# Layer one's turns without a hardware loop, a join shared by ScalarE and VectorE, and layer two's weights composed earlier

## The chip, the cores and the metric

The kernel runs on one core of one Trainium2 chip, as one program with five instruction streams: TensorE (PE; its weight loads are shown apart as PEld), VectorE (DVE), ScalarE (ACT), GpSimd (POOL) and SyncE (SP). Each engine runs its stream in order, and they meet at semaphores. The metric is the device time of one execution in microseconds (us).

## What is computed

Two message-passing layers on a graph of 3125 nodes (160 features: 64 scalars, 32 vectors of 3) and 103125 edges, sorted by target node. All is float32. Layer one, with its constants left out:

```python
h = relu(layernorm(x))
h_s, h_v = s @ lin1_ws * a, einsum(v, lin1_wv) * a       # s, v: the parts of h
w = silu(edge_scalars @ fc_w1) @ fc_w2                    # 224 weights for each edge
es, ev = h_s[edge_src], h_v[edge_src]                     # a gather for each edge
mid = [w1*es*e0, w4*(ev.e1)], [w2*es*e1, w3*ev*e0, w5*cross(ev, e1)]
agg = segment_sum(mid, edge_dst)
pre = sc(h) + agg @ lin2
x = x + [silu(pre[:, :64]), sigmoid(pre[:, 64:96]) * pre_v]
```

Layer two does without edge weights: it gathers `h = relu(layernorm(x))` by edge, multiplies with the edge's four attributes and with W1 to W5, sums by target node, applies Ws and Wv, and returns `x + (x' + relu(...))`. Since all is linear between the gather and the last relu, W1 to W5 and Ws, Wv are composed on the chip into one block of weights.

## The kernel before

**Edges.** 128 edges are a tile, 7 tiles a group, 4 groups (`UNROLL`) a turn. There are 116 groups, so 29 turns (`ITERS`), and the last group holds one tile. A stage `o` of a turn works on the turn's group `o`; some work of a stage is for the group before or after it. `stages` (line 731) sets the order for PE, ACT and DVE: two turns written out (`LEAD`), a hardware loop `Fori` over 8 rounds of three turns (`PERIOD`, the turn's place in it is the phase `p`), and three turns written out. Within the loop the number of the turn is in a register, and so are the addresses in `rel` and `sh`. POOL's stream has all turns written out already.

**Gathers.** The source rows of a tile come to `g` in one of four ways. POOL's indirect DMA (line 894) fetches most tiles, 128 rows each; it may start on a group when the products of the group four before it are done (`prod_done`). In phases 0 and 1 the last tile of group 3 is fetched row by row, by SP in one and by ACT in the other (`fetch_rows`, line 779): ACT issues `SHARES` rows behind each stage, 12 in each, but 12, 12, 8 and none in phase 1. And in layer one the last tile of groups 0 and 2 (`PICKED0`) is *found*: DVE compares the edges' source numbers with all node numbers (`match_rows`, line 1016, 128x3200), PE multiplies the match with the whole table, held as an upper and a lower half (`find0`, line 1287, 25 matmuls, to `found_at` in `sums`), and DVE adds the two halves (`join0`, line 1035, a reduction) into `g`. This happens in stages 1 and 3 of a turn (`FIND0`), 54 times in all. PE waits for the join (`found_copied`) before it aggregates into the same bank.

**A stage of layer one.** On DVE: `select` (lines 996 and 1000: the one-hot of the target within a window of 32 nodes, times the four attributes), `join0`, the products with the edge weights (lines 1087 to 1101), `name_rows` and `match_rows`, `turn` (a transpose, line 1112) and `add` (line 1133: into the accumulator `acc0`, at an address loaded from `place_i`). On PE: find, edge weights (line 1230), hidden layer (line 1216), aggregation (line 1266, 56 matmuls) and once a turn `lin2` (line 1304). On ACT: the Silu of the hidden layer (line 920), once a turn a copy of lin2's result (line 928), and then the rows of `row_part`.

**Between the layers** (`tensor_mid`, `scalar_mid`, `vector_mid`, lines 1350 to 1453), 25 tiles of nodes go through transposes (PE, line 1356, four banks), a sigmoid (ACT, line 1375), two products (DVE, lines 1405 and 1408), an addition to `X` (POOL) and statistics (DVE). Then come the normalisation, the table of layer two to DRAM, its two halves (line 1443) and `windows`. At the end DVE multiplies `pair` and `wout` with their constants (lines 1448, 1449), PE composes five planes of weights (line 1365, into the four banks) and ACT copies them to `big1_sb` (line 1394). Layer two begins on ACT with a conversion of the names (line 935), for which DVE's first matching (line 1051) waits.

**The head** loads, in SP's order, the features, later `first_rows` (which waits for 7 gathered tiles), then `pair`, `pair_k`, `wout`, `wout_k` (lines 382 to 386). On DVE `vector_self` multiplies `big0_sb` (line 552), copies from `sums` (line 555) and makes the lower half of the table (line 558, 128x4000, both operands in SBUF).

## Time and profile before

| | |
|---|---|
| median of 3 runs | 1861.78 us (1860.4 to 1862.68) |
| profiled execution | 1865.19 us, its span 1863.4 us |
| busy: PE, DVE, POOL, ACT | 1714.3, 1685.2, 1339.0, 171.4 us |
| layer one, first to last operation of DVE | 53.5 to 976.0 us |
| between the layers | to 1028.0 us |
| layer two and the output | to the end |

Times are microseconds from the span's start. A row of a timeline is: start, duration, engine, line, operation, output <- inputs, shape, count, and in brackets the idle time before it with what ended it. An engine whose row shows no idle time in brackets was busy up to it, or idle by less than 0.15 us. The "granted clock" is TensorE's. Busy time leaves out what an engine's sequencer does alone: register operations, branches, waits, issues of DMAs.

### The profile page before, as it was taken

How to read it: one execution, taken by the hardware profiler on the slowest of the kernel's cores; microseconds unless marked ns; L12 is line 12 of the kernel's file. 1: busy time of each engine (PE TensorE's matmuls, PEld its weight loads, DVE VectorE, ACT ScalarE, POOL GpSimd, SP SyncE). 2: the span in 40 equal slices, each digit the busy share in tenths (PEclk: the TensorE clock that was granted, in tenths of full speed). 3: DMA queues.
4: the chain of work that ended last, by engine and by line, in shares of the span. 5: the costliest groups of instructions: out<-in, count | busy, mean ns of one | idle time of the engine just before them, and what ended most of it. 6: DMA issues, size and time to landing. Idle time of an engine off the chain costs nothing.

```text
span 1863.4 us, 57341 instructions
## 1 busy us (share of the span) xinstructions
PE 1714.3 (92%) x15973; PEld 1488.8 (80%) x15973; DVE 1685.2 (90%) x3031; ACT 171.4 (9%) x359; POOL 1339.0 (72%) x1424
## 2 busy tenths in 40 slices
PE   8999899989898989999983899999999999999997
PEld 6677676777676767777752899999999999999997
DVE  7999899989999999999988988989898989889896
ACT  6100000000000000000005000000000000000000
POOL 4777777777777777777755777777777777777774
PEclk9899999999999999999995999999999999999999
DMA  8344443443434343434422333333333333333333
GB/s 278 105 106 108 108 110 96 107 106 98 118 91 110 102 109 103 108 91 116 112 75 86 78 84 76 83 75 84 82 76 80 83 75 82 75 81 83 74 84 90
DMA packets 109737, 181.03 MB, mean 97 GB/s; under 512 B 30072, under 2 KB 74480, under 8 KB 109248
## 3 DMA queue, kind: packets, MB, share of 16 engines
q0 software_dynamic: 66672, 113.88, 25.6%
q1 hardware_dynamic: 35592, 60.39, 10.4%
q10 hardware_dynamic: 7112, 2.94, 0.7%
q8 instruction: 106, 1.74, 0.4%
q14 instruction: 255, 2.09, 0.4%
HBM read 170.37 MB, written 6.72 MB: 95 GB/s over the span
## 4 chain that ended last, share of the span: by engine, by line
DVE 36%; PE 28%; issue 23%; ACTq 6%; DVEq 6%; DMA 1%; ACT 0%; POOL 0%; POOLq 0%
PE w_ps L1294 10%; DVE arena L1093 10%; DVE arena L1087 6%; DVE match L1051 5%; ACTq L779 5%; PE sums L1266 3%; PE sums L1270 3%; DVEq L1118 3%; PE sums L1304 3%; DVE mixed L996 3%; PE w_ps L1230 3%; DVE turned L1112 2%; PE hid_ps L1216 2%; DVE arena L1101 2%; DVE sel L1000 1%
## 5 line engine op out<-in xcount | busy, mean ns | idle before, releaser
L894 POOL DMA_INDIRECT g<-node_table,src x1382 | 1314.3, 951 | 462.1 <-issue 405.9
L1294 PE MATMUL w_ps<-split,match 128*128 128x320 f32 x3325 | 531.4, 318 | 7.9 <-DVE match L1051 7.4
L1294 PEld LDWEIGHTS w_ps<-split,match 128*128 128x128 f32 x3325 | 504.0, 193 | 12.0 <-DVE match L1051 12.0
L1051 DVE TENSOR_TENSOR match<-hid_ps,node_id_sb 128x3200 fp32r<-128x3200 f32 x105 | 361.4, 3456 | 6.9 <-ACT hid_ps L935 6.9
L1093 DVE TENSOR_TENSOR arena<-w_ps,g 128x384 f32<-128x384 f32 (+3 forms) x693 | 296.7, 455 | 2.0 <-DMA g<-node_table 1.3
L1266 PEld LDWEIGHTS sums<-arena,sel 128*32 128x32 f32 x6448 | 203.8, 111 | 116.5 <-DVE sel L1000 57.9
L1230 PE MATMUL w_ps<-fc_sb,arena 64*128 64x224 f32 x1612 | 226.9, 382 | 56.2 <-DVE arena L1087 29.5
L1000 DVE TENSOR_TENSOR sel<-mixed,sh 128x896 f32<-128x896 f32 x232 | 251.5, 1084 | 27.2
L1270 PE MATMUL sums<-g,sel 128*128 128x160 f32 x1612 | 241.5, 300 | 24.0 <-DMA g<-node_table 21.9
L1266 PE MATMUL sums<-arena,sel 128*32 128x160 f32 x6448 | 245.8, 303 | 18.0 <-DVE g L1035 17.9
L1270 PEld LDWEIGHTS sums<-g,sel 128*128 128x128 f32 x1612 | 227.2, 190 | 26.6 <-DMA g<-node_table 24.1
L1230 PEld LDWEIGHTS w_ps<-fc_sb,arena 64*128 64x128 f32 x1612 | 167.4, 193 | 100.2 <-DVE arena L1087 56.0
L1287 PE MATMUL sums<-split,match 128*128 128x320 f32 x1350 | 212.6, 313 | 0.0
L1287 PEld LDWEIGHTS sums<-split,match 128*128 128x128 f32 x1350 | 198.4, 188 | 13.6 <-issue 13.6
L1016 DVE TENSOR_TENSOR match<-mixed,node_id_sb 128x3200 fp32r<-128x3200 f32 x54 | 188.1, 3484 | 0.9
L1087 DVE TENSOR_TENSOR arena<-w_ps,g 128x256 f32<-128x256 f32 x462 | 155.6, 376 | 0.0
L1216 PE MATMUL hid_ps<-arena,fc_sb 128*128 128x512 f32 x232 | 136.2, 670 | 1.8 <-issue 1.8
L920 ACT ACTIVATE arena<-hid_ps 128x512 f32<-128x512 f32 x116 | 69.4, 598 | 740.7 <-PE hid_ps L1216 553.2
L996 DVE TENSOR_TENSOR mixed<-mixed,rel 128x224 f32<-128x224 f32 x232 | 89.4, 386 | 37.3 <-issue 30.2
L1112 DVE STREAM_TRANSPOSE turned<-sums 128x160 f32<-128x160 f32 x232 | 78.3, 338 | 26.0 <-PE sums L1304 23.1
L1051 DVE TENSOR_TENSOR match<-mixed,node_id_sb 128x3200 fp32r<-128x3200 f32 x28 | 97.8, 3492 | 1.0
L1060 DVE TENSOR_REDUCE g<-w_ps 128x160 f32<-128x320 f32 x133 | 62.5, 476 | 17.6 <-PE w_ps L1294 17.6
(113 smaller groups left out, 793.0 us busy)
## 6 DMA issues: line engine op xcount, KB each, us to landing
g<-node_table SPq DMA_DIRECT2D x2304, 0.6 KB
g<-node_table ACTq DMA_DIRECT2D x2304, 0.6 KB
arena<-edge_feat_dram SPq DMA_DIRECT2D x60, 512.0 KB
g<-node_table,src POOLq DMA_INDIRECT x1382
named<-src_rows_dram SPq DMA_DIRECT2D x30, 320.0 KB
named<-src_rows_dram SPq DMA_DIRECT2D x30, 128.0 KB
X<-x_dram SPq DMA_DIRECT2D x5, 400.0 KB, 6.5
sh<-edge_sh_dram SPq DMA_DIRECT2D x1, 1624.0 KB, 9.2
```

The lines of the kernel that those rows point to most:

```text
L894: nc.gpsimd.indirect_dma_start(out=g[:, slot(p, u, j), :], out_offset=None, in_=table[layer], in_offset=bass.IndirectOffsetOnAxis(ap=src[: ...
L1000: nc.vector.tensor_tensor(sel[:, o % 2, 0:n, :].rearrange("p t (k n) -> p t k n", k=4), hot[:, 0:n, :].unsqueeze(2).to_broadcast([P, n, 4, ...
L1016: nc.vector.tensor_tensor(match0[:], wanted0[:, i, :].unsqueeze(1).to_broadcast(wide), node_id_sb[:].unsqueeze(2).to_broadcast(wide), ALU. ...
L1051: nc.vector.tensor_tensor(match[MATCH_OF[i]][:], wanted_of[i].unsqueeze(1).to_broadcast(wide), node_id_sb[:].unsqueeze(2).to_broadcast(wid ...
L1087: return nc.vector.tensor_tensor(blocks(at), w[:, :, h * S_CH:(h + 1) * S_CH].rearrange("p t (m c) -> p t m c", m=2), rows[:, :, 0:S_CH].r ...
L1093: nc.vector.tensor_tensor(blocks(at), w[:, :, 2 * S_CH + j * V_CH:2 * S_CH + (j + 1) * V_CH].unsqueeze(2).to_broadcast([P, n, m, V_CH]), r ...
L1216: nc.tensor.matmul(hid_ps[:], fc1_sb[:], feat[:, half, within * HID:(within + 1) * HID], start=True, stop=True).then_inc(hid_done, 1)
L1230: last = nc.tensor.matmul(w_ps[:, h, part[2 * h + j] - a, 0:W_N], hid[at, o % 2, (2 * h + j) * P:(2 * h + j + 1) * P], fc2_sb[at, :], tile ...
L1266: last = nc.tensor.matmul(sums[at, o % 2, 0:width].rearrange("p (m n) -> p m n", n=WIN), sel[:, o % 2, j, at], row, tile_position=(0, k * ...
L1270: last = nc.tensor.matmul(sums[:, o % 2, 0:D], sel[:, o % 2, j, :], g[:, slot(p, o % UNROLL, j), :], **first_last)
L1287: last = nc.tensor.matmul(found_at, match0[:, t, :], split0[:, :, t, :], start=(t == 0), stop=(t == NT - 1))
L1294: last = nc.tensor.matmul(banks[:, BANK_OF[i], 0:2 * D], match[MATCH_OF[i]][:, t, :], split[:, t, :], start=(t == 0), stop=(t == NT - 1))
```

## The change

1. `WRITTEN_OUT` names layer one: `stages` writes out its 29 turns in Python for PE, ACT and DVE, with no loop inside a pass. The number of the turn and the addresses that hang on it are constants. Layer two keeps its loop. The streams grow: DVE's from 1501 to 3701 rows of the listing.
2. The join is in two parts. ACT's new `put` runs first in each stage of layer one: it waits for `found` and for the products that last read the tile's place, and copies the upper half from PSUM to `g`. DVE's `join0` waits for ACT's `upper_copied` and adds the lower half.
3. The four loads of layer two's weights are issued before `first_rows`, and DVE multiplies them in `vector_self`. PE composes one plane behind the transposes of tiles 4, 8, 12, 16 and 20 into the banks of `sums`; ACT copies each two gates later.

```diff
@@ -63,6 +63,8 @@
 PIECES = ((0, 2), (BY_ACT, 15), (2, 5), (15, 18), (5, 8), (18, 22), (8, BY_ACT), (22, NT))
 THIRD = 3
 
+COMPOSED_AT = (4, 8, 12, 16, 20)
+
@@ -88,6 +90,8 @@
 PERIODS = ITERS // PERIOD
 assert LEAD == PERIOD - 1
 ROW_TILES = (2, 2)
+
+WRITTEN_OUT = (0,)
 PARTS = (48, 48, 32)
 SHARES = ((12,) * 8 + (12, 12, 8, 0),) * 2
 AT_ONCE = 12
@@ -378,12 +382,12 @@
                 sp.wait_ge(rows_ready, b)
                 sp.dma_start(table_v[0][:, a:b, :], H[:, a:b, :]).then_inc(rows_out, 16)
             load_feat(sp, 1, 1)
-            sp.wait_ge(first_ready, RAW)
-            sp.dma_start(first_rows, g[:, 0:RAW, :].rearrange("p t c -> p (t c)")).then_inc(first_out, 16)
             sp.dma_start(pair[:], l1_pair).then_inc(pair_in, 16)
             sp.dma_start(pair_k[:], l1_pair_scale).then_inc(pair_in, 16)
             sp.dma_start(wout[:], l1_out).then_inc(pair_in, 16)
             sp.dma_start(wout_k[:], l1_out_scale).then_inc(pair_in, 16)
+            sp.wait_ge(first_ready, RAW)
+            sp.dma_start(first_rows, g[:, 0:RAW, :].rearrange("p t c -> p (t c)")).then_inc(first_out, 16)
             sp.sem_inc(first_back, 1)
             sp.wait_ge(turns_set, 1)
 
@@ -550,6 +554,9 @@
         def vector_self(dve):
             dve.wait_ge(big0_in, 32)
             nc.vector.tensor_tensor(big0_sb[:], big0_sb[:], big0_k, ALU.mult).then_inc(big0_ready, 1)
+            dve.wait_ge(pair_in, 64)
+            nc.vector.tensor_tensor(pair[:], pair[:], pair_k[:], ALU.mult)
+            nc.vector.tensor_tensor(wout[:], wout[:], wout_k[:], ALU.mult).then_inc(weights_ready, 1)
             for j, at in enumerate(CHUNK_N):
                 dve.wait_ge(sc_done[1], j + 1)
                 nc.vector.tensor_copy(acc0[:, 1, at], sums[0:S_OUT, SC_BANK[1][j], 0:at.stop - at.start]).then_inc(sc_ready[1], 1)
@@ -676,6 +683,7 @@
             late_copied = sem(L + "late_copied")
             match_done = sem(L + "match_done")
             found = sem(L + "found")
+            upper_copied = sem(L + "upper_copied")
             found_copied = sem(L + "found_copied")
             pass_of = {}
 
@@ -735,6 +743,14 @@
 
                 pass_of[eng] = r
                 q = eng.snap(ITERS * r)
+                if layer in WRITTEN_OUT:
+                    for it in range(ITERS):
+                        f = eng.snap(q + it)
+                        k, p = divmod(it - LEAD, PERIOD) if it >= LEAD else (-1, it - LEAD)
+                        e = eng.snap(PERIODS * r + max(k, 0)) - (it < LEAD)
+                        for s in range(UNROLL * it, UNROLL * (it + 1) if it < ITERS - 1 else last):
+                            stage(f, it, s - UNROLL * it, s, p, e, k)
+                    return
                 e = eng.snap(PERIODS * r + 0) - 1
                 for it in range(LEAD):
                     f = eng.snap(q + it)
@@ -927,6 +943,22 @@
                         act.wait_ge(acc_done, UNROLL * f)
                     nc.scalar.activation(lin_out, lin_ps, ACT.Copy).then_inc(lin2_copied, 1)
 
+                def put(f, o, s):
+
+                    if s == 0:
+                        act.sem_inc(upper_copied, 1)
+                    if not found0_at(o, s):
+                        return
+                    i, nxt, made = found0_at(o, s)
+                    n = NP0 * nxt + i
+                    if made:
+                        act.wait_ge(found, NP0 * f + (n + 1))
+                        act.wait_ge(prod_done, 2 * UNROLL * f + 2 * (UNROLL * nxt + PICKED0[i] + 1 - UNROLL))
+                        nc.scalar.activation(g[:, slot(-1, PICKED0[i], TILES - 1), :], found_at[:, 0, :], ACT.Copy).then_inc(upper_copied, 1)
+                    else:
+                        act.wait_ge(upper_copied, NP0 * f + n)
+                        act.sem_inc(upper_copied, 1)
+
                 def cast_early(f, nxt):
 
                     act.wait_ge(named_in[layer], 16 * f + (16 * nxt + 16))
@@ -945,7 +977,7 @@
 
                 def row_part(f, it, o, s, p, e, k):
 
-                    if ROW_TILES[layer] < 2 or o >= UNROLL or p < -1 or (p == PERIOD - 1 and s is not None):
+                    if ROW_TILES[layer] < 2 or o >= UNROLL or p < -1 or isinstance(it, int) and it == ITERS - 1:
                         return
                     part = (p + 1) % PERIOD
                     tile = e if part else e + 1
@@ -959,7 +991,9 @@
                         load_by_row(act, 1, k + 1)
 
                 def stage(f, it, o, s, p, e, k):
-                    if not own_weights:
+                    if own_weights:
+                        put(f, o, s)
+                    else:
                         if s == 0:
                             cast_early(f, 0)
                             cast_late(f, 0)
@@ -1031,9 +1065,9 @@
                     i, nxt, made = found0_at(o, s)
                     n = NP0 * nxt + i
                     if made:
-                        dve.wait_ge(found, NP0 * f + (n + 1))
-                        nc.vector.tensor_reduce(g[:, slot(-1, PICKED0[i], TILES - 1), :], found_at.rearrange("p h c -> p c h"),
-                                                AXX, ALU.add).then_inc(found_copied, 1)
+                        dve.wait_ge(upper_copied, NP0 * f + (n + 1))
+                        to = g[:, slot(-1, PICKED0[i], TILES - 1), :]
+                        nc.vector.tensor_tensor(to, to, found_at[:, 1, :], ALU.add).then_inc(found_copied, 1)
                     else:
                         dve.wait_ge(found_copied, NP0 * f + n)
                         dve.sem_inc(found_copied, 1)
@@ -1348,6 +1382,20 @@
             return e
 
 
+        def compose(pe, m):
+
+            if m == 0:
+                pe.wait_ge(weights_ready, 1)
+            if m >= 2:
+                pe.wait_ge(comp_copied, m - 1)
+            for c in range(2):
+                last = nc.tensor.matmul(sums[:, m % 2, 0:D], pair[:, 2 * m + c, :], wout[:, c, :], start=(c == 0), stop=(c == 1))
+            last.then_inc(comp_done, 1)
+
+        def composed(act, m):
+            act.wait_ge(comp_done, m + 1)
+            nc.scalar.activation(big1_sb[:, m, :], sums[:, m % 2, 0:D], ACT.Copy).then_inc(comp_copied, 1)
+
         def tensor_mid(pe):
             for t in range(NT):
                 if t >= BANKS:
@@ -1356,15 +1404,9 @@
                     last = nc.tensor.transpose(banks[:, t % BANKS, r * S_OUT:(r + 1) * S_OUT], acc0[:, r, t * P:(t + 1) * P],
                                                ident_sb[0:S_OUT, 0:S_OUT])
                 last.then_inc(node0_done, 1)
+                if t in COMPOSED_AT:
+                    compose(pe, COMPOSED_AT.index(t))
             pe.wait_ge(val_ready, NT)
-            pe.wait_ge(weights_ready, 1)
-            for m in range(PLANES[1]):
-                if m >= BANKS:
-                    pe.wait_ge(comp_copied, m - BANKS + 1)
-                for c in range(2):
-                    last = nc.tensor.matmul(banks[:, m % BANKS, 0:D], pair[:, 2 * m + c, :], wout[:, c, :],
-                                            start=(c == 0), stop=(c == 1))
-                last.then_inc(comp_done, 1)
             pe.wait_ge(comp_copied, PLANES[1])
 
         def scalar_mid(act):
@@ -1378,6 +1420,8 @@
             nc.scalar.activation(warm[:], zero[:], ACT.Sigmoid)
             for t in range(NT):
                 gate(t)
+                if t - 2 in COMPOSED_AT:
+                    composed(act, COMPOSED_AT.index(t - 2))
             root(act, parts[0], 0, var1_step, root1_done)
             act.wait_ge(norm1_ready, 1)
             root(act, parts[1], 1, var1_step, root1_done)
@@ -1389,9 +1433,6 @@
             act.wait_ge(h1_by_dve, len(by_dve))
             nc.scalar.activation(split[:, BY_ACT:, 0:D], H[:, BY_ACT:, :], ACT.Copy).then_inc(upper_ready, 1)
             nc.scalar.activation(acc[1][:, 0, :], zero[0:ROWS[1], :].to_broadcast([ROWS[1], ACC_W]), ACT.Copy).then_inc(acc1_clear, 1)
-            for m in range(PLANES[1]):
-                act.wait_ge(comp_done, m + 1)
-                nc.scalar.activation(big1_sb[:, m, :], banks[:, m % BANKS, 0:D], ACT.Copy).then_inc(comp_copied, 1)
 
         def vector_mid(dve):
             n = 0
@@ -1444,9 +1485,6 @@
             last.then_inc(split_ready, 1)
             then = Steps(dve, edge_set)
             windows(then)
-            dve.wait_ge(pair_in, 64)
-            nc.vector.tensor_tensor(pair[:], pair[:], pair_k[:], ALU.mult)
-            nc.vector.tensor_tensor(wout[:], wout[:], wout_k[:], ALU.mult).then_inc(weights_ready, 1)
             dve.wait_ge(acc1_clear, 2)
             dve.wait_ge(split_ready, 1)
             dve.wait_ge(rows1_out, 16 * len(pieces))
```

DVE in stage 1 of a turn of layer one. Before, within the loop (line 996 is the one-hot, 1035 the join, 1093 the first product):

```order
L1112 STREAM_TRANSPOSE turned<-sums 128x160 [waits l0_agg_done]
L996 ISA [waits l0_sel_done,l0_agg_done]
L996 TENSOR_TENSOR mixed<-mixed,rel 128x224
L999 REGISTER_ALU
L1000 ISA [waits l0_hot_done]
L1000 TENSOR_TENSOR sel<-mixed,sh 128x896
L1034 REGISTER_ALU
L1035 TENSOR_REDUCE g<-sums 128x160 [waits l0_found]
L1066 REGISTER_ALU
L868 ISA [waits l0_w_done]
L1093 TENSOR_TENSOR arena<-w_ps,g 128x4x96 [waits l0_gathered10]
```

After:

```order
L1146 STREAM_TRANSPOSE turned<-sums 128x160 [waits l0_agg_done]
L1030 TENSOR_TENSOR mixed<-mixed,rel 128x224 [waits l0_sel_done,l0_agg_done]
L1033 REGISTER_ALU
L1034 TENSOR_TENSOR sel<-mixed,sh 128x896 [waits l0_hot_done]
L1068 REGISTER_ALU
L1070 TENSOR_TENSOR g<-g,sums 128x160 [waits l0_upper_copied]
L1100 REGISTER_ALU
L884 ISA [waits l0_w_done]
L1127 TENSOR_TENSOR arena<-w_ps,g 128x4x96 [waits l0_gathered10]
```

The separate `ISA` ahead of the one-hot and of line 1000 are gone, and the reduction that waited for `found` is an addition that waits for `upper_copied`.

ACT at the end of stage 2's rows and the start of stage 3, before (line 779 issues a row, 920 is the Silu):

```order
L779 ISA
L779 DMA g<-node_table 1x160
L917 REGISTER_ALU
L919 REGISTER_ALU [waits l0_hid_done]
L920 ACTIVATE arena<-hid_ps 128x512 [waits l0_w_done]
L776 TENSOR_LOAD by_row
```

After (line 795 issues a row, 936 is the Silu):

```order
L795 ISA
L795 DMA g<-node_table 1x160
L955 REGISTER_ALU
L957 ACTIVATE g<-sums 128x160 [waits l0_prod_done,l0_found]
L933 REGISTER_ALU
L935 REGISTER_ALU [waits l0_hid_done]
L936 ACTIVATE arena<-hid_ps 128x512 [waits l0_w_done]
L792 TENSOR_LOAD by_row
```

The copy of the upper half (line 957) stands between the last row of the stage before and the Silu.

PE behind the last transposes between the layers, before, up to the entry of layer two:

```order
L1356 MATMUL w_ps<-ident_sb,arena 128x96 [waits val_ready]
L1356 MATMUL w_ps<-ident_sb,arena 128x96
L1365 MATMUL w_ps<-wout,pair 128x160 [waits weights_ready,val_ready]
L1365 MATMUL w_ps<-wout,pair 128x160 x7
L1365 MATMUL w_ps<-wout,pair 128x160 [waits comp_copied]
L1365 MATMUL w_ps<-wout,pair 128x160
L723 TENSOR_LOAD turns_i [waits comp_copied]
```

And after, at the first of the five compositions (line 1404 is the transpose, 1392 the composition):

```order
L1404 MATMUL w_ps<-ident_sb,arena 128x96 [waits val_ready]
L1404 MATMUL w_ps<-ident_sb,arena 128x96
L1392 MATMUL sums<-wout,pair 128x160 [waits weights_ready]
L1392 MATMUL sums<-wout,pair 128x160
L1404 MATMUL w_ps<-ident_sb,arena 128x96 [waits val_ready]
```

The ten matmuls stood together behind all transposes; now two of them stand behind the transposes of every fourth tile.

DVE in the head, after:

```order
L552 COPY mixed<-iota_sb 128x32 [waits iota_in,place_step]
L556 TENSOR_TENSOR big_sb<-big_sb,arena 128x960 [waits big0_in,place_step]
L558 TENSOR_TENSOR pair<-pair,pair_k 128x1280 [waits pair_in]
L559 TENSOR_TENSOR wout<-wout,wout_k 128x320
L562 COPY arena<-sums 96x512 [waits sc_done1] x6
L562 COPY arena<-sums 96x128 [waits sc_done1]
L565 TENSOR_TENSOR split_49<-nodes,split_49 128x4000 [waits upper0_ready,rows_out]
```

The two multiplications (lines 558 and 559) are new at this place; before, line 552's product of `big_sb` was followed at once by the copies from `sums`.

## Rows read from the trace of the kernel before

**Rows 1.** Page, busy time: us, share of the span, instructions of each engine.

```profile
PE 1714.3 (92%) x15973; PEld 1488.8 (80%) x15973; DVE 1685.2 (90%) x3031; ACT 171.4 (9%) x359; POOL 1339.0 (72%) x1424
```

**Rows 2.** Waits, DVE, 60 to 980 us: us in total, times, longest us.

```profile
DVE mixed L996 <- issue: 19.9, 6, 3.6
DVE mixed L996 <- PE sums L1266: 6.2, 18, 3.1
```

**Rows 3.** Timeline, POOL's gathers, then DVE's last full group of layer one.

```profile
33.50 0.94 POOL L894 DMA_INDIRECT g<-node_table,src  x1 [8.70 <-DMA node_table<-nodes]
...
50.10 4.27 POOL L894 DMA_INDIRECT g<-node_table,src  x1 [0.30 <-issue]
...
199.88 0.95 POOL L894 DMA_INDIRECT g<-node_table,src  x1 [0.31 <-issue]
...
333.76 0.94 POOL L894 DMA_INDIRECT g<-node_table,src  x1 [0.30 <-issue]
...
961.53 0.95 POOL L894 DMA_INDIRECT g<-node_table,src  x1 [0.30 <-issue]
...
1841.17 0.95 POOL L894 DMA_INDIRECT g<-node_table,src  x1 [0.30 <-issue]
...
972.77 0.71 DVE L1093 TENSOR_TENSOR arena<-w_ps,g 128x288 f32<-128x288 f32 x2
```

**Rows 4.** Timeline, DVE's matchings in the loop's last turn and behind it.

```profile
861.13 3.48 DVE L1016 TENSOR_TENSOR match<-mixed,node_id_sb 128x3200 fp32r<-128x3200 f32 x1
...
877.30 3.49 DVE L1016 TENSOR_TENSOR match<-mixed,node_id_sb 128x3200 fp32r<-128x3200 f32 x1
...
892.83 3.48 DVE L1016 TENSOR_TENSOR match<-mixed,node_id_sb 128x3200 fp32r<-128x3200 f32 x1
...
908.75 3.49 DVE L1016 TENSOR_TENSOR match<-mixed,node_id_sb 128x3200 fp32r<-128x3200 f32 x1
...
924.01 3.48 DVE L1016 TENSOR_TENSOR match<-mixed,node_id_sb 128x3200 fp32r<-128x3200 f32 x1
```

**Rows 5.** Groups by line and form: busy us, mean ns of one, idle before.

```profile
L1087 DVE TENSOR_TENSOR arena<-w_ps,g 128x192 f32<-128x192 f32 x230 | 70.0, 344 | 0.0
...
L1035 DVE TENSOR_REDUCE g<-sums 128x160 f32<-128x320 f32 x54 | 25.8, 479 | 0.0
...
L1394 ACT ACTIVATE nodes<-w_ps 128x160 f32<-128x160 f32 x5 | 1.5, 304 | 11.0 <-PE w_ps L1365 11.0
```

**Rows 6.** Timeline, stage 3: DVE's join and ACT's next operation, two turns.

```profile
888.63 0.48 DVE L1035 TENSOR_REDUCE g<-sums 128x160 f32<-128x320 f32 x1
...
889.28 0.60 ACT L920 ACTIVATE arena<-hid_ps 128x512 f32<-128x512 f32 x1 [5.33 <-PE hid_ps L1216]
...
919.81 0.48 DVE L1035 TENSOR_REDUCE g<-sums 128x160 f32<-128x320 f32 x1
...
921.03 0.60 ACT L920 ACTIVATE arena<-hid_ps 128x512 f32<-128x512 f32 x1 [5.63 <-PE hid_ps L1216]
```

**Rows 7.** Waits, POOL, 60 to 960 us, then 1030 us to the end.

```profile
POOL g L894 <- DVE arena L1087: 21.8, 28, 3.2
...
POOL g L894 <- PE sums L1270: 16.2, 35, 3.1
```

**Rows 8.** DMA issues: KB each, median us from issue to landing.

```profile
wout_k<-l_out_scale_dram SPq DMA_DIRECT2D x1, 160.0 KB, 8.5
...
arena<-x_node_dram,src POOLq DMA_INDIRECT x7, 3.7
```

**Rows 9.** Timeline, the head's copies, and the end of the stretch between the layers.

```profile
43.82 0.69 DVE L555 COPY arena<-sums 96x512 f32<-96x512 f32 x1 [3.61 <-PE sums L613]
...
1019.18 1.49 DVE L1448 TENSOR_TENSOR pair<-pair,pair_k 128x1280 f32<-128x1280 f32 x1
...
1021.22 4.75 PE L1365 MATMUL w_ps<-wout,pair 128*128 128x160 f32 x20 [23.12 <-DVE wout L1449]
...
1027.97 10.29 DVE L1051 TENSOR_TENSOR match<-hid_ps,node_id_sb 128x3200 fp32r<-128x3200 f32 x3 [6.89 <-ACT hid_ps L935]
```

## The prediction

> **What bounds the kernel now.** I read first the busy times of the engines: TensorE (PE) 92%, VectorE (DVE) 90%, GpSimd (POOL) 72% of the span [rows 1]. None is idle enough to be ignored, so I read who waits for whom in layer one (60 to 980 us). There DVE waits almost only for its own instruction stream: 19.9 us in 6 waits ahead of the first operation of a group (line 996), the longest 3.6 us, and one more of 3.1 us that the view books under PE [rows 2]. Those seven are the seven returns of the hardware loop. So DVE paces layer one. PE does not: nearly all of its waits there are for DVE. But POOL is nearly as close as DVE. It issues gathers back to back: from 199.88 to 333.76 us there are 107 intervals, 1.251 us each, with no gap [rows 3]. Busy 72% hides that, since the 0.30 us between two gathers are not counted. In layer two PE paces, with POOL again close behind.
>
> **Returns of the loop.** The change writes out all 29 turns, so the seven returns go: 19.9 + 3.1 = 23.0 us of idle time, less what the same operation waits anyway (the 17 other waits of the second row make 3.1 us, 0.18 each, so 1.3): **-21.7 us** on DVE. PE's and ACT's own returns lie beside DVE's.
>
> **Registers.** In the loop, the addresses of `rel` and `sh` come from a register, and an extra instruction stands ahead of lines 996 and 1000. The trace has one ordinary turn written out already, the first of the three that stand behind the loop. From matching to matching (line 1016) the loop takes 16.17 + 15.53 = 31.70 us a turn, and the written-out turn 15.92 + 15.26 = 31.18 us [rows 4]. 24 turns leave the loop: 24 x 0.52 = **-12.5 us** on DVE.
>
> **The join.** DVE's reduction of 128x320 takes 479 ns. It becomes an addition of 128x160. A product of 192 columns takes 344 ns [rows 5], so I take 0.31 us at 160 columns: 0.17 us less, 54 times, **-9.2 us** on DVE.
>
> **The wait that comes with the join.** DVE no longer waits for PE's `found`, which is 2.5 us old by then, but for ACT's copy. ACT works in order, and its copy stands behind the twelve row loads of the stage before. In stage 3 these end late: the next operation of ACT starts at 889.28 in a loop turn where DVE's join starts at 888.63; in the written-out turn it is 921.03 against 919.81 [rows 6]. The new copy takes the place of that operation. A copy of 128x160 out of PSUM takes 0.30 us [rows 5]. So the join would come 889.28 + 0.30 - 888.63 = 0.95 us late at the loop's pace, 1.2 us once DVE is 0.27 us faster between its two joins, and 921.03 + 0.30 - 919.81 = 1.5 us by the written-out turn. I take 1.4. It happens where stage 2 has twelve rows: in turns 1 to 26, except the nine of phase 1, which have eight rows there, so 18 times: **+25 us** (22 to 27). Stage 1's join has over 2 us to spare, since find ends well before it and the rows end at about the same time as find. Queued behind DVE's wait are the products of that group; PE waits for them. That makes the join's move a loss by itself, since 25 is more than 9.2.
>
> **DVE's path through layer one:** -21.7 - 12.5 - 9.2 + 25.2 = -18.2 us.
>
> **POOL's path.** The layer has 727 gathers, the first at 33.50, the last at 961.53 [rows 3]. 726 x 1.2512 = 908.4 us, so 19.6 of the 928.0 us are lost: 3.3 in the gather of 4.27 us at 50.10, 0.3 in one before it, and 16 in waits for buffers that DVE frees late (28 of them are booked under DVE, the longest 3.2 us [rows 7]). A faster DVE gives back these 16 us at most. The last full group's last gather then starts at about 945, and lands 3.7 us later by the first gathers of the program [rows 8], at 949. DVE's products of it start at 972.77 now [rows 3]. So POOL allows -23.8 us and no more: of the 43.4 us that DVE alone would save, 20 are not to be had whatever ACT does. DVE's -18.2 ends later, so it counts.
>
> **The head.** DVE now multiplies `pair` and `wout` (1.49 and 0.48 us, as the same operations take at 1019 us [rows 9]) ahead of the copies that start at 43.82 [rows 9]. The last of the four loads lands 8.5 us after its issue [rows 8]; issued behind the feature load, from 31.6 on, it lands at some 42.3, so DVE is free at 44.3: **+0.5 us** (0 to 3). The other effect is on POOL: the gather at 50.10 took 4.27 us instead of 0.95, while DVE ran one addition of 128x4000 with both operands in SBUF. The two multiplications are of that kind, so I count 1.0 us (0.3 to 1.7) for POOL, which is already in the 945 above. The Trainium skill ("SBUF — State Buffer", section "Who interferes with whom") says that a tensor_tensor with both inputs in SBUF contends only with GpSimd's reads and was not seen to stall descriptor generation; by that the 1.0 us would be nothing. The row at 50.10 speaks against it, and it would not change the path that ends last.
>
> **Between the layers.** Now DVE multiplies at 1019.18, PE composes, ACT copies, and only then does ACT convert the names for which DVE's first matching waits: it starts at 1027.97 [rows 9]. After the change ACT is free before DVE is, and DVE is free after its windows at 1019.2, so the first matching starts at about 1019.5: -8.5 us. The five compositions lie among 25 gates, where DVE paces and PE waits for DVE in every tile; each puts 4.75 / 5 = 0.95 us on PE [rows 9], which has a lead of three tiles: +0.3 us (0 to 1.5). Layer two, however, has the same floor: POOL starts as before, waits for PE 16.2 us in 35 waits [rows 7], of which 0.30 each is its ordinary gap, so 5.7 us can be given back, and 0.4 for the multiplication that slowed a gather at 1020. Its last gather starts at 1841.17 [rows 3], just ahead of the last full aggregation. So between 6.1 and 8.5: I take **-7.3 us**.
>
> **Sum:** -18.2 + 0.5 + 0.3 - 7.3 = -24.7 us. The profiled execution took 1865.19 us (span 1863.4), the median of the runs is 1861.78. The sum is made on the profile and taken from the median: **1837 us**.
>
> **Rivals.**
> *A, POOL paces.* ACT's copy isn't late, or only so little that DVE's path falls under POOL's. For it: at the loop's pace the lateness is 0.95 us, and below 1.1 us POOL's floor decides. Against it: the written-out turn shows more. Time: 1861.8 - 23.8 + 0.3 - 7.3 = 1831; with all of the 8.5 us, 1830.
> *B, ACT is later than I read.* When DVE waits for ACT and ACT's rows wait for PE, a delay can be handed round. With 2.2 us for each of 18 joins, layer one gives -43.4 + 40 = -3.8, and the whole -10: 1851.
> *C, slower.* The copy queues not only behind the rows but, in stage 1 too, behind the Silu that waits for PE. The point is 18 x w = 43.4 + 6.5 + 3.7, w = 3.0 us; at 3.3 us the time is 1861.8 - 43.4 + 59.4 - 6.5 = 1871. Against it: ACT's rows never end more than 1.3 us after the join in these rows.
> *D, the long code isn't free.* Streaming four times as many instructions stalls the engines and gives back the returns: around 1858, no difference that can be told. Against it: the tail's turn and POOL, whose code is written out already and whose interval never varies.
>
> **How the numbers follow.** My forecast (1832 to 1845) has 0.50, A with less than 1832 0.25, B 0.15, D 0.04, C 0.04, and 0.02 for a gain below both floors. 1828 to 1849 takes in the first two, the bounds of the unknown costs (ACT 22 to 27, between the layers 6.1 to 8.5, the head 0 to 3) and half of B. A measurement of this kernel tells 0.2% (3.7 us) from no change: faster 0.91, same 0.04, slower 0.05.
>
> **What would show it.** Idle time of 3 us ahead of DVE's first operation of a group is gone; a turn takes about 32.2 us where twelve rows precede and 30.8 elsewhere; DVE's addition waits for ACT some 18 times for 1.2 to 1.6 us; POOL waits for DVE next to nothing and its last gather of layer one starts at 946 to 950. If DVE instead waits for gathers in most turns, A holds. DVE's first matching of layer two follows its windows within 1 us, and the compositions are nowhere waited for. The forecast is wrong if a stall stands in the middle of written-out code, or if stage 1's addition waits too.

## Result and the profile after

The changed kernel takes 1837.83 us (median of 4 runs, 1834.34 to 1844.54), the kernel before 1861.68 us (4 runs, 1860.4 to 1862.68): a ratio of 0.9877, 95% interval 0.9848 to 0.9905. Run again beside other kernels it took 1838.46 us (below). 1837 was forecast.

The profiled execution of after took 1834.34 us, its span is 1832.4, so it is 31.0 us shorter than the profiled one of before, while the medians differ by 23.9. After's is the fastest of its runs, before's is slower than its other ones. The stages have to be compared with that in mind, and further down it matters.

The page of after, busy times, which answer to [rows 1]:

```profile
PE 1693.8 (92%) x15973; PEld 1477.0 (81%) x15973; DVE 1674.9 (91%) x3031; ACT 184.4 (10%) x413; POOL 1339.8 (73%) x1424
```

The shares say next to nothing: DVE is 91% busy instead of 90%. The waits say it. DVE from 60 to 960 us (us in total, times, longest), to be set against [rows 2]:

```profile
DVE g L1070 <- ACT g L957: 25.2, 18, 1.7
DVE arena L1167 <- DVE arena L1167: 4.6, 27, 0.5
DVE arena L1167 <- issue: 2.0, 3, 1.5
...
DVE arena L1127 <- DMA g<-node_table: 1.1, 1, 1.1
...
DVE mixed L1030 <- PE sums L1300: 0.3, 1, 0.3
```

The seven waits of 3 us ahead of the first operation of a group are gone. In their place stands the addition (line 1070), which waits 18 times for ScalarE's copy (line 957), 25.2 us in all. The costs of the join itself, by line and form (busy us, mean ns of one, idle before):

```profile
L1070 DVE TENSOR_TENSOR g<-g,sums 128x160 f32<-128x160 f32 x54 | 17.0, 315 | 25.5 <-ACT g L957 25.2
L957 ACT ACTIVATE g<-sums 128x160 f32<-128x160 f32 x54 | 16.4, 304 | 284.6 <-issue 129.9 <-PE sums L1321 127.4 <-DVE arena L1121 27.4
```

The turn, read from DVE's matchings in the timeline (start, duration), to be set against [rows 4]:

```profile
396.75 3.48 DVE L1050 TENSOR_TENSOR match<-mixed,node_id_sb 128x3200 fp32r<-128x3200 f32 x1
412.34 3.49 DVE L1050 TENSOR_TENSOR match<-mixed,node_id_sb 128x3200 fp32r<-128x3200 f32 x1
429.13 3.48 DVE L1050 TENSOR_TENSOR match<-mixed,node_id_sb 128x3200 fp32r<-128x3200 f32 x1
444.72 3.49 DVE L1050 TENSOR_TENSOR match<-mixed,node_id_sb 128x3200 fp32r<-128x3200 f32 x1
459.82 3.48 DVE L1050 TENSOR_TENSOR match<-mixed,node_id_sb 128x3200 fp32r<-128x3200 f32 x1
475.41 3.49 DVE L1050 TENSOR_TENSOR match<-mixed,node_id_sb 128x3200 fp32r<-128x3200 f32 x1
```

396.75 to 429.13 is a turn with twelve row loads ahead of the late copy, 32.4 us (32.2 forecast); 444.72 to 475.41 is one with eight, 30.7 us (30.8 forecast).

GpSimd no longer waits in layer one. All 26 entries below are its ordinary gap of 0.3 us, where [rows 7] had waits of up to 3.2:

```profile
POOL g L910 <- DVE arena L1121: 7.9, 26, 0.3
```

Timeline of after: GpSimd's gather beside DVE's long addition in the head, its last of layer one, its first and last of layer two; DVE's last full group of layer one, the first product of the gates, and the first matching of layer two. They answer to [rows 3] and [rows 9]:

```profile
48.80 5.40 POOL L910 DMA_INDIRECT g<-node_table,src  x1 [0.31 <-issue]
...
946.60 0.95 POOL L910 DMA_INDIRECT g<-node_table,src  x1 [0.30 <-issue]
992.61 1.68 POOL L910 DMA_INDIRECT g<-node_table,src  x1 [9.48 <-DMA node_table<-nodes]
...
1813.20 0.95 POOL L910 DMA_INDIRECT g<-node_table,src  x1 [0.30 <-issue]
...
952.70 0.71 DVE L1127 TENSOR_TENSOR arena<-w_ps,g 128x288 f32<-128x288 f32 x2
...
962.85 0.28 DVE L1446 SCALAR_TENSOR_TENSOR val<-w_ps,a_col,sig 128x64 f32<-128x64 f32 x1 [0.90 <-PE w_ps L1404]
...
999.86 10.29 DVE L1085 TENSOR_TENSOR match<-hid_ps,node_id_sb 128x3200 fp32r<-128x3200 f32 x3 [0.93 <-DVE place_i L539]
```

**Where the 31.0 us of the two profiled executions went.** The first product of the gates starts at 983.24 before and 962.85 after: layer one gave 20.4. From there the first matching of layer two follows after 44.73 us before and 37.01 after: the early composition gave 7.7. From that matching to the last gather both need 813 us (1027.97 to 1841.17, 999.86 to 1813.20). The last 3.0 us lie behind the last gather, and all of them ahead of the transposes of the output (before, then after; TensorE's rows from the last gather on):

```profile
1841.85 2.14 PE L1270 MATMUL sums<-g,sel 128*128 128x160 f32 x14 [0.67 <-DVE turned L1112]
1845.44 2.44 PE L1270 MATMUL sums<-g,sel 128*128 128x160 f32 x16 [1.45 <-DVE sel L1000]
...
1853.61 6.30 PE L1477 MATMUL w_ps<-ident_sb,nodes 80*128 80x80 f32 x50 [2.88 <-DVE nodes L1133]
```

```profile
1814.54 2.42 PE L1304 MATMUL sums<-g,sel 128*128 128x160 f32 x8 [2.22 <-DMA g<-node_table,src]
...
1822.69 4.92 PE L1515 MATMUL w_ps<-ident_sb,nodes 80*128 80x80 f32 x50 [2.57 <-DVE nodes L1167]
```

When the last gather starts, TensorE has 30 matmuls of aggregation left before and 8 after, so the transposes start 12.4 us behind it before and 9.5 after. They took 6.30 and 4.92 us, at a mean granted clock of 0.57 and 0.64 of full speed in ten microseconds, but that doesn't set the end: from their start to the end of the span it is 9.8 and 9.7 us, and in dve_join (below), where they took 6.29 us, 9.7 as well. In the two other kernels with the late composition they also start over 12 us behind the last gather (12.3 and 12.4), in those with the early one 9.1 to 11.2. So these 3 us belong to layer two's part of the change, which gave 10.6 in all between these two executions.

### The profile page after: what moved, and what is told of

It is laid out like the page before. It is cut to its first block, busy times and chain, and to the rows that moved or that the text cites. A ratio compares the mean times of both kernels' runs of the same rounds, so it can differ in the third digit from the quotient of the medians.

```text
span 1832.4 us, 57154 instructions
## 1 busy us (share of the span) xinstructions
PE 1693.8 (92%) x15973; PEld 1477.0 (81%) x15973; DVE 1674.9 (91%) x3031; ACT 184.4 (10%) x413; POOL 1339.8 (73%) x1424
## 4 chain that ended last, share of the span: by engine, by line
PE 29%; DVE 25%; issue 21%; ACTq 16%; DVEq 4%; ACT 2%; DMA 2%; POOL 1%; POOLq 0%
ACTq L795 13%; PE w_ps L1328 11%; DVE arena L1127 6%; DVE match L1085 5%; PE sums L1338 5%; PE sums L1300 4%; PE sums L1304 4%; DVE arena L1121 3%; ACTq L792 2%; DVEq L1152 2%; PE w_ps L1264 2%; DVE mixed L1030 2%; PE hid_ps L1250 2%; DVE turned L1146 2%; DVE arena L1135 1%
## 5 line engine op out<-in xcount | busy, mean ns | idle before, releaser
L1264 PE MATMUL w_ps<-fc_sb,arena 64*128 64x224 f32 x1612 | 221.0, 373 | 34.6 <-DVE arena L1121 31.1
L1304 PEld LDWEIGHTS sums<-g,sel 128*128 128x128 f32 x1612 | 227.9, 191 | 27.3 <-DMA g<-node_table 22.1
L1264 PEld LDWEIGHTS w_ps<-fc_sb,arena 64*128 64x128 f32 x1612 | 161.3, 187 | 78.3 <-DVE arena L1121 59.7
L1250 PE MATMUL hid_ps<-arena,fc_sb 128*128 128x512 f32 x232 | 131.5, 649 | 1.8 <-issue 1.8
L944 ACT ACTIVATE lin_sb<-sums 96x256 f32<-96x256 f32 (+1 forms) x58 | 22.1, 381 | 561.7 <-PE sums L1338 455.8
```

The lines of the kernel that those rows point to most:

```text
L1264: last = nc.tensor.matmul(w_ps[:, h, part[2 * h + j] - a, 0:W_N], hid[at, o % 2, (2 * h + j) * P:(2 * h + j + 1) * P], fc2_sb[at, :], tile ...
L1304: last = nc.tensor.matmul(sums[:, o % 2, 0:D], sel[:, o % 2, j, :], g[:, slot(p, o % UNROLL, j), :], **first_last)
```

## Experiments

Each is the changed kernel with one edit, or two. Times are medians; ratios are to the kernel before, run on the same chip beside it. "The copy waits" are the waits of DVE's line for ScalarE's copy in layer one.

| kernel | us | ratio (95%) | copy waits | first gate product | from there to the end |
|---|---|---|---|---|---|
| before | 1861.68 | 1 | none | 983.24 | 880.2 |
| after | 1837.83 | 0.9877 (0.9848 to 0.9905) | 25.2, 18 times | 962.85 | 869.6 |
| after_again | 1838.46 | 0.9875 (0.9852 to 0.9897) | 25.4, 18 | 963.39 | 870.8 |
| dve_join | 1833.66 | 0.9847 (0.9828 to 0.9866) | none | 959.55 | 869.4 |
| copy_between | 1830.41 | 0.9829 (0.9807 to 0.9851) | none | 957.63 | 870.8 |
| compose_late | 1840.12 | 0.9878 (0.9859 to 0.9897) | 25.6, 18 | 968.25 | 876.4 |
| dve_join_compose_late | 1834.43 | 0.9847 (0.9820 to 0.9873) | none | 957.06 | 874.9 |
| loop_kept | 1869.68 | 1.0044 (1.0027 to 1.0062) | 21.2, 18 | 999.39 | 870.5 |
| compose_only | 1857.29 | 0.9969 (0.9958 to 0.9980) | none | 985.55 | 870.8 |
| fewer_gathers_act | 1839.96 | 0.9881 (0.9867 to 0.9896) | 25.2, 18 | 966.66 | 870.8 |
| fewer_gathers_dve | 1817.95 | 0.9763 (0.9749 to 0.9778) | none | 945.68 | 869.2 |
| copy_between_fewer | 1811.74 | 0.9729 (0.9703 to 0.9756) | none | 937.68 | 871.0 |
| rows_spread | 1923.13 | 1.0332 (1.0306 to 1.0357) | 96.1, 41 | 1049.08 | 869.7 |
| rows_even | 1863.35 | 1.0002 (0.9994 to 1.0011) | 8.0, 12 | 988.65 | 870.8 |

The last two columns are of the profiled execution of each. The first gate product contains the head, whose length differs between executions: DVE's first matching starts anywhere from 64.05 to 67.7 us. Differences of 1 or 2 us in that column say nothing by themselves.

### The join, undone

```
-    dve.wait_ge(upper_copied, NP0 * f + (n + 1))
-    nc.vector.tensor_tensor(to, to, found_at[:, 1, :], ALU.add)
+    dve.wait_ge(found, NP0 * f + (n + 1))
+    nc.vector.tensor_reduce(to, found_at.rearrange("p h c -> p c h"), AXX, ALU.add)
```

> After with the join put back to VectorE: one reduction of both halves (479 ns), no copy by ScalarE; all else as after. My theory: the 25.2 us of waits for ScalarE's copy go and 54 x 0.17 = 9.2 us of longer joins come, so VectorE alone would be 16 us earlier; but GpSimd issued its gathers without one wait and its last gather of layer one starts at 946.60, landing at about 951.3, and VectorE's last full group starts at 952.70. So only 1 to 2.5 us are to be had: about 1836 us beside after's 1837.8, the last gather again at 946 to 947, and VectorE now waiting for gathers in most turns. Rival 1, GpSimd is no limit: 16 us faster, about 1822. Rival 2, the waits for the copy were not on the path: 0 to 9 us slower, 1838 to 1847.

1833.66 us, 4.2 less than after. DVE's waits from 60 to 955 us:

```profile
DVE arena L1125 <- DMA g<-node_table,src: 11.5, 12, 2.4
DVE arena L1165 <- DVE arena L1165: 4.7, 28, 0.5
DVE arena L1165 <- issue: 2.5, 2, 1.5
DVE arena L1125 <- issue: 2.4, 2, 1.9
```

The waits for the copy went, and waits for gathers came. Most of the gain stuck at GpSimd, as forecast; it was some 2 us more than I allowed. Part of the reason is that a gather releases its reader sooner than the 3.7 us after its start that I had taken from the program's first gathers [rows 8]. Timeline of GpSimd and DVE:

```profile
933.44 0.94 POOL L910 DMA_INDIRECT g<-node_table,src  x1 [0.30 <-issue]
...
936.03 0.89 DVE L1125 TENSOR_TENSOR arena<-w_ps,g 128x384 f32<-128x384 f32 x2 [1.56 <-DMA g<-node_table,src]
...
937.19 0.95 POOL L910 DMA_INDIRECT g<-node_table,src  x1 [0.30 <-issue]
...
940.62 0.72 DVE L1125 TENSOR_TENSOR arena<-w_ps,g 128x288 f32<-128x288 f32 x2 [2.38 <-DMA g<-node_table,src]
```

The last group has one gather and the group before it seven, so, counted back from the last one at 947.20, 933.44 is the fourth gather of group 113 and 937.19 its seventh. The products at 936.03 wait for the fourth and those at 940.62 for the seventh: 2.59 and 3.43 us. In copy_between (below) the same count gives 2.66 us for the layer's last full group, from 944.89 to 947.55.

### Who paces: fewer gathers

```
     own = [j for j in range(max(a, skip), min(b, n)) if j not in others]
+    if own_weights and it and u == 1 and h == 0:
+        own = own[1:]
```

The same edit in the changed kernel and in dve_join. The messages of 28 tiles are computed from old rows.

> After, leaving out one gather in each turn of layer one but the first (28 of 727; the messages of those tiles are computed from old rows), so that GpSimd needs 28 x 1.2512 = 35.0 us less. My theory: the waits for ScalarE's copy pace layer one, GpSimd doesn't, so the time stays at after's: 1835 to 1839, 25 us of waits for the copy as before. Rival, GpSimd paces: VectorE ends earlier by more than 5 us, below 1833.

> The kernel with VectorE's own join, leaving out the same 28 gathers. My theory: there GpSimd paces (VectorE waits 12 times for gathers, 11.5 us in all, at one gather each 1.2512 us); without them these waits go and VectorE paces by its own work alone: 11 to 12 us less, 1822. Rival, the waits for gathers lie beside other work: 1833.7 as before.

With ScalarE's copy: 1839.96 us, nothing gained from 35 us less of gathers, and the row of waits stays the same:

```profile
DVE g L1072 <- ACT g L959: 25.2, 18, 1.6
```

With VectorE's own join: 1817.95 us, 15.7 less than with all gathers. That is more than the 11.5 us of waits under one name; with the 2.4 booked as issue it is 13.9, and the gates start 13.9 us earlier (945.68 against 959.55). So the copy paces layer one of the changed kernel, and with the copy gone GpSimd does. These four kernels are the clearest answer of the study.

### Loop and composition apart

```
-WRITTEN_OUT = (0,)
+WRITTEN_OUT = ()
```

> After with the hardware loop over layer one's turns kept; the join on two engines and the early composition stay. My theory: the returns (21.7) and the registers (12.5) come back, 34.2 us on VectorE; its waits for ScalarE's copy are a little shorter at the slower pace (0.95 to 1.2 us instead of 1.4, 18 times), 4 to 8 us less. So 26 to 30 us slower than after: 1864 to 1868, above the kernel before (1861.7), and GpSimd waits for VectorE again. Rival, the waits for the copy vanish at the loop's pace: 34.2 - 25.2 = 9 us slower than after, 1847.

1869.68 us, 31.8 more than after and slower than before, a little above the 1864 to 1868 expected. The copy waits shrank to 21.2 us only, so the rival (they vanish at the loop's pace) is out.

The loop, and VectorE's own join as well, so that the early composition alone is left of the change:

> The kernel before with the early composition alone: loop and VectorE's own join stay. My theory: the first matching of layer two starts 37.0 us after the first gate's product instead of 44.7, so 7.7 us early, and layer two can take them since GpSimd ran there 828.3 us from first gather to last where its floor is 820.3: 1861.1 - 7.7 = 1853.5. Rival: GpSimd is the floor and had little to give back, so only 2 us are kept (the kernel with all but the early composition lost no more than that): 1859. And against it stands the join's move in the loop: the kernel with loop, ScalarE's copy and early composition took 1869.7, so the move costs 16 us there by my theory (21.2 us of waits less 9.2 would be 12).

1857.29 us, ratio 0.9969: 5.0 us less than the kernel before on the same chip (1862.3), by the interval 3.7 to 7.8. It lies between the two expectations. The loop with ScalarE's copy against the loop without it, 1.0044 against 0.9969, is 14 us for the join's move in the loop, near the 12 from 21.2 of waits less 9.2.

The late composition in the changed kernel, and in dve_join; the edit puts the diff's lines back where they were:

> After with layer two's weights multiplied and composed where they were before: behind VectorE's windows, in banks of their own. My theory: the first matching of layer two starts 7 to 8 us later behind the gates (999.86 in after, 44.7 us after the first gate's product instead of 37.0), and TensorE keeps that loss to the end: 1845 us beside 1837.8. Rival, GpSimd's floor: its gathers of layer two start when the table is written, whatever the composition does, and ran in after without a wait, so layer two takes the loss back and the time is within 2 us of after's: under 1840.

> Written out, with VectorE's own join and the late composition: what the early composition is worth in the fastest kernel so far (1833.7). Two bounds stand from earlier kernels. The first matching starts 7.7 us later behind the gates; if TensorE keeps that to the end, 1841. GpSimd needed 824.4 us for layer two's gathers with the late composition and 820.3 with the early one; if that is what counts, 4 us, 1838. If GpSimd's floor hides the composition, 1834 to 1836.

1840.12 and 1834.43 us. By the medians the late composition costs 2.3 and 0.8 us, less than 7 in both, but the intervals allow 5 either way, so the medians don't settle it. The last column of the table is sharper. It is 874.9 and 876.4 us in these two, and 869.2 to 871.0 in all eleven executions with the early composition (870.3 in the mean). So it is worth 4.6 to 6.1 us from the gates on, not 7.7 in full, and compose_only's 5.0 by medians agrees. The first matching is 7.7 us late (44.68 us behind the first gate product instead of 37.0), and GpSimd's gathers then give back a part: with the early composition GpSimd needs 820.3 us from its first gather of layer two to its last, its floor; with the late one the last gather starts 809.5 and 808.3 us after the first matching instead of 813. The stretch behind the last gather, 22.1 us instead of 19.2 to 20.9, takes part of that again, since TensorE is further behind. In the one execution of before it was 813.2 us, and 880.2 from the gates on: nothing given back. From the first matching to the last gather TensorE was busy for 785.5 us there (784.3 and 782.5 in the two kernels with the late composition), and in layer two it waited 7.4 us for matchings (5.5 in both) and 21.9 us for the tiles fetched row by row (20.4 and 20.9). Together that covers the difference of 3.7 and 4.9 us; why it was so in that execution stays open.

### Is it the row loads? Two kernels that went wrong, and one that went right

```
-SHARES = ((12,) * 8 + (12, 12, 8, 0),) * 2
+SHARES = ((13, 13, 8, 13) * 2 + (13, 13, 8, 0), (12,) * 8 + (12, 12, 8, 0))
-AT_ONCE = 12
+AT_ONCE = 13
```

> After with ScalarE's row loads dealt out otherwise in layer one: 13 in each stage but stage 2, which has 8 in every turn (the last stage none), instead of 12 everywhere but one stage of 8. My theory: the copy of stage 3 stood late because of the twelve loads ahead of it, so its 18 waits go (in phase 1, with eight loads, there was none in after), VectorE keeps its cheaper addition, and GpSimd paces: 1836 us, like the kernel with VectorE's own join, the last gather at 946 to 947. Rival 1, the thirteenth load moves the wait to stage 1's join: no gain or slower, 1838 to 1845. Rival 2, the lateness has another cause than the loads: 25 us of waits stay, 1838.

1923.13 us, 85 more than after. None of the theories had this. ScalarE's timeline (with its DMA issues, ACTq), first of after, then of this kernel:

```profile
513.52 0.60 ACT L936 ACTIVATE arena<-hid_ps 128x512 f32<-128x512 f32 x1 [5.58 <-issue]
514.65 4.64 ACTq L795 DMA_DIRECT2D g<-node_table  x12
519.46 0.30 ACT L957 ACTIVATE g<-sums 128x160 f32<-128x160 f32 x1 [5.33 <-issue]
```

```profile
528.80 0.59 ACT L936 ACTIVATE arena<-hid_ps 128x512 f32<-128x512 f32 x1
531.93 4.96 ACTq L795 DMA_DIRECT2D g<-node_table  x13
537.10 0.60 ACT L936 ACTIVATE arena<-hid_ps 128x512 f32<-128x512 f32 x1 [7.71 <-issue]
```

The thirteenth load costs 0.3 us. But from the end of the Silu to the first load pass 2.54 us instead of 0.53. In between lies the load of the row numbers into registers. What counts is where the numbers start, and this kernel shows it by itself: ahead of 8 loads the gap is 1.52 us where the stage starts at row 26, and 0.30 where it starts at row 120, a multiple of four. Ahead of 13 loads behind ScalarE's copy of lin2's result it is 2.79 us from row 13 and 0.98 from row 60. That these gaps make the 85 us is the likely account; no run with 13 loads and all starts at multiples of four was made.

```
-SHARES = ((12,) * 8 + (12, 12, 8, 0),) * 2
+SHARES = ((12, 12, 8, 12) * 2 + (12, 12, 8, 8), (12,) * 8 + (12, 12, 8, 0))
```

> After with eight row loads in stage 2 of every turn and twelve in the others (eight in the last stage of three turns); all offsets stay multiples of four. In the kernel with 13 and 8 loads, ScalarE spent 2.5 us ahead of a first load at an offset like 34 and 1.5 us at 26, where it spends 0.5 in after, so that kernel said nothing on the lateness. My theory: the copy of stage 3 is late because ScalarE works without a gap from stage 1's twelve loads to stage 2's; with eight there the 18 waits of 1.4 us go, the addition stays cheap and GpSimd paces, with VectorE waiting for gathers a dozen times: 1833 to 1835 us, as with VectorE's own join (1833.7). Rival, the lateness doesn't come from the loads, or wanders to another stage: 15 us of waits or more stay, 1837 to 1840.

1863.35 us, 25 more than after. DVE's waits from 60 to 955 us:

```profile
DVE arena L1127 <- DMA g<-node_table: 35.9, 8, 4.7
DVE g L1070 <- ACT g L957: 8.0, 12, 1.1
```

The copy waits fell from 25.2 to 8.0 us, which fits the loads as the cause. But the edit was a bad one: it moved the last eight loads of a tile from stage 2 into stage 3, whose products read that tile, and DVE now waits for their landing, 4.5 us in each of eight turns, and 5.3 in a ninth behind this window. Those waits give ScalarE time as well. That is my mistake, and neither the time nor the smaller waits settle the theory.

The third kernel leaves every load where it is and moves the copy:

```
     part of stage 2:
-    fetch_rows(act, mybir.EngineType.Activation, 1, a, b)
+    fetch_rows(act, mybir.EngineType.Activation, 1, a, a + 4)
+    put(f, 3, s + 1)
+    fetch_rows(act, mybir.EngineType.Activation, 1, a + 4, b)
```

> After with ScalarE's copy for stage 3 taken out from behind stage 2's row loads and put between them: four loads, the copy, then the other eight (with a register load of their own). TensorE's found is there at 516.19 in a turn where four loads end at 516.2 and the addition could start at 518.55. My theory: the place of the copy, behind the loads, made the wait. So the 18 waits of 1.4 us go, the cheap addition stays, and GpSimd paces: 1833 to 1835 us, as with VectorE's own join, with a dozen waits of VectorE for gathers. Rival: ScalarE has no gap between stages 1 and 2, so the 0.3 us of the copy and the 0.5 us of the second register load come out at the Silu behind the loads, 0.8 us in each of 26 turns: no better than after, 1837 to 1845.

1830.41 us (1829.86 to 1831.9), the fastest that computes everything, 7.4 less than after and 3 under what was expected. Timeline of ScalarE, and of DVE's addition:

```profile
505.65 0.30 ACT L957 ACTIVATE g<-sums 128x160 f32<-128x160 f32 x1 [2.11 <-PE sums L1329]
506.53 3.40 ACTq L795 DMA_DIRECT2D g<-node_table  x8
...
507.93 0.31 DVE L1078 TENSOR_TENSOR g<-g,sums 128x160 f32<-128x160 f32 x1
```

The copy now waits for TensorE's find, which is what it is there for, and ends 2 us before the addition, which waits for nothing. DVE's waits of layer one are now for gathers:

```profile
DVE arena L1135 <- DMA g<-node_table,src: 19.8, 22, 2.4
```

So the place of the copy behind the loads made the wait, and GpSimd paces once it is gone.

> The same with 28 gathers of layer one left out, so that GpSimd paces no longer. My theory: the kernel with VectorE's own join and as many gathers took 1817.95 us; the join on two engines saves 54 x 0.17 = 9.2 us of VectorE if ScalarE's copy is in time, so 1809. Rival, ScalarE becomes the bound: 1818 or more.

1811.74 us (1809 expected), 6.2 less than fewer_gathers_dve. The gates start at 937.68 instead of 945.68, 7.8 us earlier when both are counted from DVE's first matching (65.34 and 65.50). An ordinary turn, from matching to matching:

```profile
402.47 3.49 DVE L1060 TENSOR_TENSOR match<-mixed,node_id_sb 128x3200 fp32r<-128x3200 f32 x1
...
433.15 3.49 DVE L1060 TENSOR_TENSOR match<-mixed,node_id_sb 128x3200 fp32r<-128x3200 f32 x1
```

That is 30.68 us, and 31.03 in fewer_gathers_dve (406.51 to 437.54): 0.35 a turn, 0.17 for each of its two joins. So inside the turns the join on two engines brings all of the 9.2 us that the durations promise, when the copy is in time and GpSimd is out of the way. 7.8 reach the gates, and 6.2 the medians.

### The changed kernel again

> The changed kernel itself once more, beside the others of this set, since its first four runs lie 10 us apart (1834.3 to 1844.5) while TensorE's mean granted clock ran from 0.977 to 0.971. If the spread comes from the clock's dips, which fall anew in each run, the times order by the mean clock again, and the median is 1836 to 1840 us. If it comes from a race between ScalarE's copy and VectorE, times at one clock lie as far apart as times at different clocks.

1838.46 us (1835.97 to 1840.4). After's first four runs order by TensorE's mean granted clock: 1834.34 at 0.977, 1837.38 at 0.975, 1838.27 at 0.973, 1844.54 at 0.971. The five new ones don't: 1838.46 at 0.979, 1835.97 and 1840.4 at 0.973. Over nine runs the spread is 10 us; copy_between's five lie within 2.0 us at 0.972 to 0.980. So the mean clock is not enough to explain it. Nor does the pace by ScalarE's copy explain it: the four runs of fewer_gathers_act, which has the same 18 waits, lie within 1.9 us. The cause of the spread stays open.

## Why the prediction held, step by step

**The wait that comes with the join** was right to the digit: 25.2 us in 18 waits. The reason holds too: with the copy between the loads they are gone.

**Returns and registers** were too small together. Without the copy and without GpSimd as a bound, the gates start at 945.68 instead of 983.24: 37.6 us earlier, 38.3 if both are counted from DVE's first matching (65.50 and 64.80). I had 34.2. The term at fault is the registers. The returns were right: the seven turns that hold one take 34.66 to 35.15 us, together 21.9 us more than seven of 31.70 (21.7 forecast). Matchings in the loop of the kernel before, and two of dve_join, one turn apart each:

```profile
453.13 3.49 DVE L1016 TENSOR_TENSOR match<-mixed,node_id_sb 128x3200 fp32r<-128x3200 f32 x1
...
484.83 3.49 DVE L1016 TENSOR_TENSOR match<-mixed,node_id_sb 128x3200 fp32r<-128x3200 f32 x1
...
519.70 3.49 DVE L1016 TENSOR_TENSOR match<-mixed,node_id_sb 128x3200 fp32r<-128x3200 f32 x1
```

```profile
406.52 3.49 DVE L1048 TENSOR_TENSOR match<-mixed,node_id_sb 128x3200 fp32r<-128x3200 f32 x1
...
437.53 3.49 DVE L1048 TENSOR_TENSOR match<-mixed,node_id_sb 128x3200 fp32r<-128x3200 f32 x1
```

A written-out turn takes 31.01 us, not the 31.18 that the one turn behind the loop showed [rows 4]; against the loop's 31.70 that is 24 x 0.69 = 16.6, not 12.5. The turn from 484.83 to 519.70, 34.87 us, is one of the seven with a return.

**The join** was 0.17 us shorter each time, as taken, and brought that in every turn. Of the 9.2 us, 7.8 reached the gates where nothing else bounded the layer.

**DVE's path.** From the terms as measured, -38.3 - 7.8 + 25.2 = -20.9; the trace gives -20.4, or -19.8 from the first matching. The forecast was -18.2. It was 4.1 us short on the registers and 1.4 us over on the join, and the 1 us between sum and trace is not accounted for.

**GpSimd's floor.** The last gather of layer one starts at 946.60 (946 to 950 forecast), and in layer one it never waits. The floor of -23.8 put DVE's last full group at 949.0; in dve_join it starts at 949.02, not held by its gather, and in copy_between, released by its gather, at 947.55. Counted from the first gather (33.50 before, 33.14 in copy_between) that is 914.4 us instead of 915.5, so the floor was 1.1 us roomier than worked out: the gather released its reader after 2.66 us instead of 3.7. With the copy's wait removed, layer one ended 3.3 us (dve_join) and 5.2 us (copy_between) earlier, 4.5 and 5.1 if all are counted from the first gather. Rival A, GpSimd as the pace, thus came true in the experiments, once the copy was in time, and with a time (1830.4) near the 1830 to 1831 given for it.

**The head.** First matching at 64.22 instead of 64.80: the +0.5 didn't come. DVE multiplied `pair` from 39.95 on without a wait, so the loads were there over 2 us sooner than the 42.3 taken, and both products were done 1.8 us ahead of the first copy. Over all kernels the first matching starts anywhere from 64.05 to 67.7 us, with or without the two multiplications. GpSimd did lose time. Beside DVE's multiplications two gathers took 1.36 and 1.10 us instead of 0.95 (one before, 1.27), and the gather beside the long addition took 5.40 instead of 4.27: 5.0 us lost instead of 3.6, so 1.4 more (1.0 forecast). It now starts before the addition, at 48.80 against 49.06, and stands until that is over. In every kernel looked at a gather that meets this addition ends 0.8 us behind it. The Trainium skill ("SBUF — State Buffer", section "Who interferes with whom") says that such an operation was not seen to stall descriptor generation; in the traces here a gather is held up beside it, in all 14 profiles, and they decide. The gathers also read their row numbers (`src`) from SBUF, and no run separates that reading from the writing of descriptors.

**Between the layers** the first matching follows DVE's windows and one cast by 0.93 us, and the stretch is 7.7 us shorter (8.2 forecast). Gates and compositions: TensorE waits 3.3 us for DVE there, and for no composition.

**Layer two** was to take back up to 2.4 of the 8.5 us, 1.2 by my choice, so that 7.0 were left for everything from the gates on. Measured in comparable kernels it is 4.6 to 6.1: the first matching comes 7.7 us early, and 1.6 to 3.1 are taken back. This term was too large by 1 to 2.4 us, about what layer one's was too small. In the two profiled executions alone it would read 10.6, which is why the comparison of those two traces, by itself, would have misled.

**The total** is closer than its terms. 1837.83 against 1837 is a miss of under 1 us, while the registers were 4 us too small, and the join and layer two too large by 1.4 and 1 to 2.4 us. What is shown is the mechanism and the size of the wait; that the sum fits to a microsecond is luck.

**The other rivals.** B, ScalarE later than read: no, 1.4 us a time. C, slower: the wait was never above 1.7 us and its point was 3.0; stage 1's addition never waited. But with the loop kept the join's move made the kernel slower than before, 1869.7 us; it is a loss of its own, as the sum said. D, the long code: no stall stands inside it.

## What to carry to other kernels

When an operation is handed to a lightly used engine, look at what is queued ahead of it there at that very moment, not at the engine's busy share: ScalarE was 10% busy by its operations, and the twelve DMA issues ahead of the copy cost 25 us. Then move the copy between them, not the loads. And before counting a saving on one engine, compute the floor of the next one by its interval (1.25 us a gather), not by its busy time (0.95).

## What I had not expected of the hardware

- Loading row numbers into ScalarE's registers took 0.3 us for eight numbers from an offset that is a multiple of four, 1.5 us for eight and 2.5 us for thirteen from other offsets. The kernel with thirteen rows in most stages, mostly from such offsets, took 85 us more.
- A gather that starts just before a 128x4000 addition in SBUF takes 5.40 us, one that starts 0.86 us into it 4.27; both end 0.8 us behind it.
- Written out, a turn took 0.69 us less on DVE, a third more than the tail's turn of the same kernel had shown.
